# Attention block and mixture of experts on one core: the MLP starts two steps earlier, the routing reads its slots with maxima, the weights' preparation puts v first, and the end adds its two buffers on TensorE

## The reference

```python
xn = _layernorm(x)
# branch 1: gated linear attention, then an MLP
q, k, v = rms @ Wq, rms @ Wk * s, rms @ Wv;  g = rms @ Wg + bg      # rms = rmsnorm(xn, ln1_w)
gk = log_sigmoid(rms @ Wkg1 @ Wkg2 + bkg2) / 16
S = S * exp(gt)[..., None] + kt[..., None] * vt[..., None, :]       # 512 steps, 16 heads, 8 x 16
ot = einsum('bhk,bhkd->bhd', qt, S)
s = xn + (silu(g) * headnorm(o)) @ Wo
s = s + silu(rms2 @ W1) * (rms2 @ W3) @ W2                          # hidden 704
# branch 2: the best 4 of 16 experts, softmax weights, hidden 224
top_w, top_idx = top_k(softmax(xn @ router_w.T + expert_bias), 4)
g = silu(sum_k top_w[k] * down(silu(gate(xn)) * up(xn)))
out = x + s * g
```

## Time and profile before

| | |
|---|---|
| time, median of 3 runs | 574.86 us (572.45 to 577.04) |
| profiled execution | 574.92 us, span 572.9 us |
| PE busy | 429.3 us (75%) |
| DVE busy | 345.0 us (60%) |
| POOL busy | 304.7 us (53%) |
| ACT busy | 230.9 us (40%) |
| chain of work that ended last | PE 54%, DVE 19%, issue 9%, DMA 8%, POOL 4% |
| DMA | 90.42 MB, 158 GB/s over the span |

### The profile page before, as it was taken

One profiled execution on the slowest core, in us unless ns is written; L12 is line 12 of the kernel. 1 busy time (PEld: TensorE's weight loads), 2 busy tenths in 40 slices (PEclk: granted clock), 3 DMA queues, 4 the chain that ended last, 5 costly groups with the idle time before them and its releaser, 6 DMA issues.

```text
span 572.9 us, 8861 instructions
## 1 busy us (share of the span) xinstructions
PE 429.3 (75%) x2170; PEld 254.9 (44%) x2171; DVE 345.0 (60%) x613; ACT 230.9 (40%) x521; POOL 304.7 (53%) x230
## 2 busy tenths in 40 slices
PE   2479970313568798699889989999999999999400
PEld 1134320101223354255465557767767767677200
DVE  4665867999989979985755633333333333333065
ACT  0526642300133132122554525556655656566221
POOL 4052695146768468576720006656566656666535
PEclk9989996655759899899999999999999999999855
DMA  8334998745535234232988845666666666664493
GB/s 265 110 111 160 304 330 279 270 150 171 186 123 185 89 126 151 106 114 65 357 288 238 176 149 85 112 101 114 103 112 112 112 102 110 111 85 57 55 318 121
DMA packets 78616, 90.42 MB, mean 158 GB/s; under 512 B 7704, under 2 KB 66808, under 8 KB 78584
## 3 DMA queue, kind: packets, MB, share of 16 engines
q1 hardware_dynamic: 47584, 54.82, 31.6%
q0 software_dynamic: 14592, 19.47, 20.0%
q10 hardware_dynamic: 16408, 15.73, 8.5%
HBM read 50.66 MB, written 39.34 MB: 157 GB/s over the span
## 4 chain that ended last, share of the span: by engine, by line
PE 54%; DVE 19%; issue 9%; DMA 8%; POOL 4%; ACT 2%; ACTq 2%; SPq 0%; POOLq 0%; DVEq 0%
PE mm_ps L315 33%; PE sum_ps L315 12%; DVE st L959 4%; PE turn_ps L1276 3%; DVE kv L951 3%; PE mm_ps L1374 3%; POOL qs L529 2%; DMA rows_scratch<-zrow 2%; DMA eb<-n_L_ffn_expert_bias_dram 2%; PE sum_ps L1247 2%; DVE w_gu L1181 2%; DMA vrep<-v_scratch 1%; DMA y_scratch<-y,X 1%; ACTq L636 1%; DVE ghead L1111 1%
## 5 line engine op out<-in xcount | busy, mean ns | idle before, releaser
L586 POOL DMA_INDIRECT y_scratch<-y,X x80 | 124.3, 1554 | 126.7 <-ACT y L815 96.6
L315 PE MATMUL mm_ps<-w_gu,xT 128*128 x480 | 103.9, 352 | 1.6 <-DVEq L1159 1.5
L529 POOL TENSOR_TENSOR qs<-st,q_sb 128x1024 f32<-128x1024 f32 x32 | 75.4, 2356 | 49.0 <-DVE st L959 24.3
L1071 DVE TENSOR_TENSOR xT<-turn_ps,xT 128x256 f16<-128x256 f32 x80 | 33.9, 425 | 88.0 <-ACT xT L726 88.0
L315 PE MATMUL sum_ps<-wd,hT 112*128 x320 | 82.4, 380 | 0.0
L558 POOL DMA_INDIRECT rows_scratch<-rows,slot_u x64 | 64.0, 1001 | 27.2 <-issue 15.1
L959 DVE TENSOR_TENSOR_SCAN st<-sum_ps,kv 128x512 f32<-128x512 f32 x64 | 75.1, 1210 | 1.0
L315 PE MATMUL mm_ps<-an2T,w 128*128 128x512 f16 x264 | 65.1, 403 | 13.6 <-DVE h_mlp L1080 11.1
L1247 PE MATMUL sum_ps<-qs,sumk 128*32 128x512 f32 x128 | 38.2, 710 | 38.5 <-POOL qs L529 37.2
L315 PEld LDWEIGHTS mm_ps<-w_gu,xT 128*128 128x128 f16 x480 | 46.6, 97 | 33.0 <-issue 2.7
L1164 DVE SCALAR_TENSOR_TENSOR h<-mm_ps,X,sl 128x224 f32<-128x224 f32 x80 | 36.1, 451 | 40.9 <-ACT sl L799 40.9
(11 more groups left out here) (165 smaller groups left out, 533.4 us busy)
## 6 DMA issues: line engine op xcount, KB each, us to landing
vrep<-v_scratch SPq DMA_DIRECT2D x64, 256.0 KB
rows_scratch<-zrow ACTq DMA_DIRECT2D x16, 685.0 KB, 11.7
X<-rows_scratch SPq DMA_DIRECT2D x80, 137.0 KB, 2.6
w_gu<-y_scratch SPq DMA_DIRECT2D x16, 256.0 KB, 6.1
y_scratch<-zrow ACTq DMA_DIRECT2D x6, 640.0 KB, 5.9
w_gu<-in_L_ffn_gate_proj_dram SPq DMA_DIRECT2D x16, 224.0 KB, 6.8
w_gu<-in_L_ffn_up_proj_dram SPq DMA_DIRECT2D x16, 224.0 KB, 7.1
wd<-in_L_ffn_down_proj_dram SPq DMA_DIRECT2D x1, 3136.0 KB, 17.4
```

What stands on the lines that cost most here:

```text
L315: last = nc.tensor.matmul(out_ap, lhsT, rhs, start=(n == 0), stop=(n == len(pairs) - 1))
L529: nc.gpsimd.tensor_tensor(qs[:, u % 2, :, :], st[:, u % 2, :, :], pair_bc(q_sb[:, TOK(a)]), ALU.mult).then_inc(s["qs_ready"], 1)
L586: nc.gpsimd.indirect_dma_start(y_dram[u % 2], bass.IndirectOffsetOnAxis(ap=X[:, u, TOKEN_C:TOKEN_C + 1].bitcast(U32), axis=0), y[:, u, :], ...
L1071: nc.vector.tensor_tensor(xT[:, u % 2, 1, :, :].rearrange("p c n -> p (c n)"), PS[u % 2][:, 0:KC * P], xT[:, u % 2, 0, :, :].rearrange("p ...
```

## The change

Seven things are changed together.

1. **Start.** The loads are in another order (Wv, Wq, Wk, Wg, x of batch 1, then the small ones), each wait names what it needs (`wv_in`, `wqk_in`, `wg_in`, `ln1_in`, `bz_in`, `bg_in`, `late_in`) where before one semaphore stood for six small loads. v0 and v1 are the first outputs, ScalarE moves them out of PSUM (VectorE did), and TensorE waits for the parts that an output needs (`LOW_PARTS`). Statistics and scales of batches 2 and 3 move from the start into steps 0 and 1 of pass 0, their normed rows on GpSimd too.
2. **Pass 0.** All eight steps of batch 0 stand there; the 24 outputs are spread over 8 steps. The fill of `rows_scratch` is 8 DMAs of 128 pieces of 10,960 bytes from a wide tile `wide` that lies in `w13`.
3. **Routing in pass 1.** `route_scores` in step 0, `route_choice` in step 2, `route_slots` in step 4; the reduce for the maximum goes (column 0 of `m8` is used); the slots are read by 16 MAX8 over `slot * Msel`; the owner of a tile is found with tiles on partitions, turned by TensorE and copied (`name_tiles`). MLP weights are prepared in steps 0 to 5 of pass 1 (`w13` is free only after the fill). Scatters begin in step 6 of pass 1, two or three a step.
4. **Steps of b.** Head norm in step 1, gate product in 2, output projection in 3, second norm in 4, its turned parts in 5 (before: 2 and 3, 4, 5 and 6, 6 and 7, 7).
5. **MLP from step 6 on.** c's m = 0 and 1 run in steps 6 and 7 of the pass in which c was b. Pass 5 has six steps.
6. **79 tiles.** At most 79 tiles can be in use, so the 80th isn't computed.
7. **End.** Four pieces of buffer 1 are loaded before buffer 0 is complete; TensorE adds the buffers by matmuls with the identity into eight PSUM banks, ScalarE takes silu from there, VectorE multiplies and adds x.

```diff
-        STEP_ENDS = [7, 11, 14, 17, 20, 24, 24, 24]
+        STEP_ENDS = [4, 7, 10, 13, 16, 19, 22, 24]
...
+        MLP_FROM = 6
+
         def turns(eng, step_fn):
 
             batch = lambda i: i if 0 <= i < B else None
             for it in range(1, B + 2):
-                for u in range(U):
-                    step_fn(batch(it), batch(it - 1), batch(it - 2), u)
+                for u in range(U if it <= B else MLP_FROM):
+                    c, m = (it - 1, u - MLP_FROM) if u >= MLP_FROM else (it - 2, u + U - MLP_FROM)
+                    step_fn(batch(it), batch(it - 1), batch(c), m, u, (it - B) * U + u)
...
+            sp.wait_ge(s["eg_ready"], USED_TILES + 2)
+            sp.wait_ge(y_out[1], 16 * (USED_TILES // 2))
+            for c in range(PIECES // 2):
+                load_sum(1, c)
+            sp.wait_ge(y_out[0], 16 * (USED_TILES - USED_TILES // 2))
             for c in range(PIECES):
...
+                load_sum(0, c)
+                if c < PIECES // 2:
+                    load_sum(1, c + PIECES // 2)
...
+                if u == 0:
+                    pool.wait_ge(s["ln_ready"], 3)
+                if u < 2:
+                    for t in range((u + 2) * TPB, (u + 3) * TPB):
+                        normed_rows(t)
...
+                if b == 0 and u < 3 * KC:
+                    mlp_weights(u // 3, u % 3)
+                if b == 0 and u == 3 * KC - 1:
+                    pool.sem_inc(s["prep_done"], 1)
...
+            def fill_rows(i):
+                act.dma_start(rows_dram[i * P * WIDE:(i + 1) * P * WIDE].rearrange("(p n) c -> p (n c)", p=P), wide)\
+                    .then_inc(s["zero_fill"], 16)
...
+                if i in (V0_OUT, V1_OUT):
+                    c = i - V0_OUT
+                    act.wait_ge(vt_out[c], 16 * (p + 1))
+                    nc.scalar.activation(vt[:, c, :], bank_of(p, i), ACT.Copy).then_inc(s["vt_ready"], 1)
...
-            FIRST = 6
+            FIRST = U
 
             for u in range(FIRST):
                 for _ in recurrence(0, u):
                     pass
+                if u == 0:
+                    row_scales(TPB, 2 * TPB)
+                    statistics(2)
+                    statistics(3)
+                if u == 1:
+                    scales(2 * TPB, NT, 6 * TPB)
+                    row_scales(2 * TPB, NT)
...
+                step(nc.vector.tensor_tensor(slot[:, :, :], slot[:, :, :], Msel[:, :, :], ALU.mult))
+                for t in range(NT):
+                    nc.vector.max(s8[:, t, :], slot[:, t, :]).then_inc(s["dve_max"], 1)
...
+            def step_fn(a, b, c, m, u, n):
+                split_low(experts_at(n - 1)[-1:])
+                if b == 0 and u == 5:
+                    low_of_turned(b)
+                if a is not None:
+                    for ahead in {0: (0, 1), 1: ()}.get(u, (u,)):
                         for _ in recurrence(a, ahead):
                             pass
...
+                if c and u == MLP_FROM:
+                    add_mlp(c - 1, 1)
...
+            def add_piece(i, c):
+                pe.wait_ge(x_in[PIECES * i + c], 16 * GROUPS + 16)
+                ins = nc.tensor.matmul(SUM_BANKS[c], ident[:, :], (ysum, ysum2)[i][c], start=(i == 1), stop=(i == 0))
```

More of the change, by code:

```diff
@@ L521, in _ @@
             pool.wait_ge(s["ln_ready"], 2)
-            for t in range(TPB, NT):
+            for t in range(TPB, 2 * TPB):
                 normed_rows(t)
@@ L1177, in _ @@
             tiles(GROUPS - 1, True)
-            def scaled(c):
+            dve.wait_ge(s["xr_in"], 16)
+            for c in range(PIECES):
                 dve.wait_ge(s["silu_ready"], c + 1)
```

667 lines of the change are left out of this document (346 added, 321 removed).

## The result

| | before | after |
|---|---|---|
| time, median of 4 runs each | 573.65 us (571.86 to 577.04) | 587.01 us (585.08 to 588.37) |
| profiled execution, span | 572.9 us | 586.4 us |
| PE, DVE, ACT, POOL busy | 429.3, 345.0, 230.9, 304.7 us | 460.8, 332.5, 233.5, 293.0 us |
| mean granted clock of TensorE | 0.897 | 0.888 |

The changed kernel is slower: the ratio is 1.0223, with a 95% interval of 1.0163 to 1.0284, so 1.6 to 2.8% longer. VectorE does 12.5 us less work, as meant. TensorE's busy time grew by 31.5 us although it has one tile less. 15.4 of them are the new sums at the end (32 matmuls).

A forecast was written before the change was run, and what follows sets the result against it. It took VectorE to bound routing and passes 1 to 3, TensorE the tiles. Terms -4.9 + 0 + 3.8 - 6.2 - 2.4 - 2.4 = -12.1 from 574.92 gave 562.8, stated as 562.5 us, range 547 to 572.

The forecast's parts named there:

- Start: Up to the first `kv`: first output at about 16 us, `kv` at 35.8 instead of 40.67, so -4.9 us.
- first `kv` of pass 1 at about 88: End of pass 0: TensorE ends near 86, ScalarE refills K, and the pass takes 52 us.
- Pass 1: Pass with the routing: 73 us, from 57 of VectorE's work, 6 of port waits, 7 before the gated product, 3 small.
- Rival C: Pass 1: GpSimd's products and weights hold the routing's two-source instructions 0.7 us each; +20 us, 582.5 us; chance 0.08.
- the term of +3.8: Passes 2 and 3: same work moved against each other, 51.3 and 50.5 us against 49.7 and 48.3.
- 3 us before the gated product: Step 6 of passes 2 and 3: VectorE idles 3 us while TensorE starts the new batch, where a recurrence covered it.
- The output projection's second half 1 us late: Passes 2 and 3: the second half of the output projection comes 1 us late.
- The walk to the MLP's start: Passes 4 and 5, last batch's chain from pass 3's last scan to its MLP: 36.6 us against 43.3.
- That part stays, plus 0.5: From the MLP's start to the first tile: 29.3 us stay, plus 0.5 for the first rows' split behind `add_mlp`.
- Tiles and end: From the first tile on: -2.4 us for 79 tiles and -2.4 beyond it at the end, 4.8 ahead.
- Rival B: End: TensorE stays at 1.2 GHz, 16 sums at 1.9 us; +11, so 573.5 us, no change; chance 0.11.
- Rival A: Passes 0 to 3: the waits put into the sum are mostly covered; -14, so 548 us; chance 0.27.

The follow-up runs named there:

- Narrow_fill: Changed kernel with the eight fills of rows_scratch written as rows of 1,096 bytes, not pieces of 10,960: 602.87 us, kernel before 585.63 beside it.
- early_fill: Changed kernel with three of eight filling DMAs in step 0 of pass 0, none in steps 6 and 7: 579.46 us, kernel before 574.30, ratio 1.0064.
- after_third: The changed kernel itself, run again without an edit, in the group where the kernel before takes 573.02 us: 585.32 us, one execution.
- Wo_first: Changed kernel with the output projection ahead of step 2's read-out on TensorE in step 3 of each pass: 596.01 us, kernel before 585.63.
- gated_later: Changed kernel with the first two gated products of each batch's MLP one recurrence later on VectorE: 592.95 us, kernel before 585.63.
- best_order: Changed kernel with early_fill, Wo_first, gated_later, experts' splits spread, the last splits ahead of the MLP's last additions: 558.21 us, kernel before 573.02, ratio 0.9747.

## Why the prediction was wrong, point by point

- **Start: right, -6.0 for -4.9.** The first output starts at 16.08 (about 16), GpSimd's rows at 30.07 (31.3), the first `kv` at 34.69 (35.8).
- **Pass 0: wrong.** The step "first `kv` of pass 1 at about 88", after 52 us, counted only TensorE's outputs. It measured 63.3 us. TensorE's gap was there (6.67 us before the turning at 50.71) and its last output ended at 88.6, not far from the 86 of the sum, but the change to the fill was costed at its memset alone, and what its pieces do to the loads of v behind them was not asked. VectorE waited 16.1 us for v. Narrow_fill (5.0 us) and early_fill (9.5 us) showed most of these waits to be the fill's, and early_fill's pass 0 took 56.5 us (63.3 in after, 59.5 in after_third).
- **Pass 1: right in its parts.** 69.6 us for 73. The wait before the first gated product is 6.7 us (7), behind GpSimd's 2.84 us of weights. The routing's instructions were held for 5.0 us (6), `grow` beside them for another 3.2. The longest stood beside weights of GpSimd's, in the timeline of after:

```profile
105.78 1.32 DVE L1063 MAX8 m<-lg 128x8 f32<-128x16 f32 x16
118.38 1.70 DVE L1071 TENSOR_TENSOR gt<-lg,m 128x256 f32<-128x256 f32 x1
120.12 2.96 DVE L1072 TENSOR_TENSOR eq<-lg,m 128x256 f32<-128x256 f32 x1
...
119.75 3.03 POOL L579 TENSOR_TENSOR w<-w_raw,w 128x1408 f16<-128x1408 f32 x1
```

  `eq` has two inputs and took 2.96 us, where instructions of its size take 0.42; MAX8 beside a product took 1.32 (1.30 in the earlier trace rows). By the Trainium skill ("GPSIMD Engine Reference", section 1, Specifications) instructions with two inputs in SBUF contend with GpSimd for the shared interfaces, and the trace agrees. Rival C's mechanism is real, a few us in size. That pass 1 came out 3.4 us under the forecast made the sum of passes 0 and 1 look better than its first term was.
- **Passes 2 and 3: the term of +3.8 was mis-sized, it measured +17.7.** (Its own items add up to +2.8 a pass, 5.6 in all; the sum took 1.6 and 2.2.) 12 us of it are waits. Its 3 us before the gated product were 2.9. "The output projection's second half 1 us late" was 3.7: the step looked at the gated head output and not at what stands ahead of the projection on TensorE, nor at the clock after such a wait. The additional 1.0 stands behind the second half of W2, which took 7.43 us (209.86, above) where both halves in before took 6.03 and 5.93. Another 4 us are one more instruction per pass held by GpSimd's product, where less port waiting had been forecast; in before `grow` stood clear of it. The rest, 1.4 us, is not traced. Wo_first and gated_later took back 8.0 and 9.1 us, and in best_order, together, 15.8. In VectorE's and GpSimd's timelines of after, pass 2:

```profile
203.38 2.28 DVE L267 TENSOR_SCALAR grow<-grow 128x4 int32<-128x4 int32 x1
...
203.29 2.34 POOL L569 TENSOR_TENSOR qs<-st,q_sb 128x1024 f32<-128x1024 f32 x1 [3.42 <-DVE st L1030]
```

- **Passes 4 and 5: one half right, one wrong.** The walk to the MLP's start was 37.2 us for 36.6 (its steps as listed add up to 36.4). "That part stays, plus 0.5", of the 29.3 us behind it, failed: 37.7 us, of which 8.4 are the wait before W2 and W2's slow clock. The sum followed the batch's own chain, and the experts' splits, whose table the change had also to press into two steps fewer, weren't in it.
- **Tiles and end: -8.2 for -4.8.** From the first tile to the loads of the buffers 203.2 us for 206.9, of which 2.4 are the tile. From there to the end 25.1 us for 29.6. The sums took two at 1.7 us and fourteen at 0.86, where three at 1.9 and 13 at 0.95 had been forecast; the last store lands 2.5 us behind VectorE, not 4.45. In the timeline of after:

```profile
564.97 3.39 PE L1492 MATMUL turn_ps<-w_gu,ident 128*128 128x512 f32 x4 [9.44 <-DMA w_gu<-y_scratch]
568.20 1.88 PE L1492 MATMUL mm_ps<-w_gu,ident 128*128 128x512 f32 x4
...
583.18 0.69 DVE L1259 TENSOR_TENSOR w_gu<-w_gu,xback 128x512 f32<-128x512 f32 x1
```

  Rival B fell: the clock came back after the second sum (granted clock 0.55 from 564.9 to 568.2, 1.00 from there to 580.5).
- **The chances.** Slower had 0.08, all of it for a mechanism that measured 5 us in the routing, less than the sum already held. The three real losses (fill against v, projection behind read-out, splits behind each other) were in no rival. Rival A, 548 us, assumed that the new waits are covered; with the order mended many of them are, at 558, which is 4.6 us less than the 562.8 of the sum. So the idea of the change was sound, and its order of instructions was not.

## What to carry to other kernels

When a change shortens a pass, everything that was spread over its steps (transfers, splits, scatters) is pressed into fewer: lay each such stream's own pace, here 2.16 us for an expert and 1.37 MB for a fill, against the new step, and not only the chain that the change is about. Put what is ready ahead of what must wait for another engine in TensorE's program: here idle stretches of 2.9 to 4.8 us were paid twice, once as idling and once at the slow clock behind them. Where two DMA queues share the engines, look at the size of the other queue's pieces, not only at its bytes: the same fill made VectorE wait 16.1 us for v in pieces of 10,960 bytes and 5.0 us in rows of 1,096.
